# The expert gate is spread over the ranks by DMAs on the GpSimd queue in place of a matmul

## The reference

```python
def cond(x, weight, adapter_ids):                 # x: 8 sequences of 256 tokens, 1024 wide
    w = weight[adapter_ids]
    return jnp.einsum('bsi,boi->bso', x, w)

def ffn(x, W_base, b_base, W_router, A_stack, B_stack):
    xf = x.reshape(-1, 1024)
    probs = jax.nn.softmax(xf @ W_router.T, axis=-1)              # 8 experts
    topk_p, topk_i = jax.lax.top_k(probs, 2)
    topk_p = topk_p / jnp.sum(topk_p, axis=-1, keepdims=True)
    combine = jnp.sum(jax.nn.one_hot(topk_i, 8) * topk_p[..., None], axis=1)
    h = jnp.einsum('nd,erd->ner', xf, A_stack)                    # rank 16
    h = h * combine[..., None]
    lora_out = jnp.einsum('ner,eor->no', h, B_stack) * 2.0
    return xf @ W_base.T + b_base + lora_out

out = x + ffn(cond(x, cond_weight, ids), W_base, b_base, W_router, A_stack, B_stack)
```

## Time and profile before

| | us |
|---|---|
| median of 3 runs | 396.14 |
| lowest to highest | 395.95 to 396.31 |
| the profiled execution | 396.64 |
| its span, first to last instruction | 394.9 |
| PE busy | 389.8 (99%) |
| DVE busy | 306.1 (78%) |
| ACT busy | 183.9 (47%) |

### The profile page before, as it was taken

One profiled execution on the slowest core, in us unless ns is written; L12 is line 12 of the kernel. 1 busy time (PEld: TensorE's weight loads), 2 busy tenths in 40 slices (PEclk: granted clock), 3 DMA queues, 4 the chain that ended last, 5 costly groups with the idle time before them and its releaser, 6 DMA issues.

```text
span 394.9 us, 5710 instructions
## 1 busy us (share of the span) xinstructions
PE 389.8 (99%) x2189; PEld 332.8 (84%) x2189; DVE 306.1 (78%) x443; ACT 183.9 (47%) x282; POOL 40.1 (10%) x68
## 2 busy tenths in 40 slices
PE   7999999999999999999999999999999999999997
PEld 6888888888888888888888888888888888888886
DVE  4897967789699999984547786878867999999322
ACT  5877734749542334332146676357656223441000
POOL 0101100101000130021162000000000001301110
DMA  7998782768430136486669967347173102461222
GB/s 249 405 358 287 261 309 86 265 230 289 166 106 0 53 110 196 165 288 229 198 228 365 349 236 251 108 164 217 46 258 112 58 0 81 151 197 75 87 80 80
DMA packets 21227, 72.96 MB, mean 185 GB/s; under 512 B 2832, under 2 KB 3104, under 8 KB 21200
## 3 DMA queue, kind: packets, MB, share of 16 engines
q1 hardware_dynamic: 15984, 55.58, 40.8%
q0 software_dynamic: 4928, 15.97, 11.3%
q10 hardware_dynamic: 288, 1.05, 0.7%
HBM read 64.20 MB, written 8.39 MB: 184 GB/s over the span
## 4 chain that ended last, share of the span: by engine, by line
PE 97%; DMA 1%; SPq 1%; ACT 0%; issue 0%; DVE 0%
PE bank_x L829 30%; PE bank_x L833 15%; PE bank_y L814 9%; PE bank_y L815 8%; PE bank_y L816 8%; PE bank_x L816 8%; PE bank_x L814 8%; PE bank_x L815 8%; PE bank_y L873 2%; DMA raw<-w_cond 1%; SPq L368 1%; PE bank_y L893 0%; ACT wc_hl L501 0%; SPq L352 0%; DVE out_sb L606 0%
## 5 line engine op out<-in xcount | busy, mean ns | idle before, releaser
L829 PE MATMUL bank_x<-x_hl,wc_hl 128*128 128x512 f32 x512 | 128.7, 393 | 1.2 <-ACT wc_hl L501 1.2
L547 DVE TENSOR_TENSOR wc_hl<-raw,wc_hl 128x1024 fp32r<-128x1024 f32 x90 | 108.4, 1220 | 18.9 <-ACT wc_hl L483 18.8
L483 ACT CAST wc_hl<-raw 128x1024 fp32r<-128x1024 f32 x90 | 93.4, 1051 | 55.7 <-DVE raw L551 23.1
L829 PEld LDWEIGHTS bank_x<-x_hl,wc_hl 128*128 128x128 f32 x512 | 92.3, 189 | 18.3 <-ACT wc_hl L501 1.8
L833 PEld LDWEIGHTS bank_x<-x_hl,wc_hl 128*128 128x128 f32 x512 | 70.0, 190 | 5.1
L833 PE MATMUL bank_x<-x_hl,wc_hl 128*128 128x256 f32 x512 | 71.5, 282 | 0.0
L435 POOL DMA_DIRECT2D out<-out_sb x28 | 15.3, 545 | 249.8 <-DVE out_sb L598 228.5
L515 ACT COPY xc_low<-bank_x 128x256 f32<-128x256 f32 x64 | 23.6, 369 | 32.4 <-PE bank_x L833 32.3
L814 PE MATMUL bank_x<-x_hl,wc_hl 128*128 128x512 f32 x96 | 37.4, 389 | 0.0
L815 PE MATMUL bank_x<-x_hl,wc_hl 128*128 128x512 f32 x96 | 37.4, 389 | 0.0
L816 PE MATMUL bank_x<-x_hl,wc_hl 128*128 128x512 f32 x96 | 37.4, 389 | 0.0
(11 more groups left out here) (93 smaller groups left out, 492.8 us busy)
## 6 DMA issues: line engine op xcount, KB each, us to landing
raw<-w_cond SPq DMA_DIRECT2D x62, 512.0 KB, 4.9
raw<-w_base SPq DMA_DIRECT2D x24, 512.0 KB, 5.3
out_sb<-x POOLq DMA_DIRECT2D x32, 256.0 KB, 5.3
raw<-x SPq DMA_DIRECT2D x14, 512.0 KB, 4.6
out<-out_sb POOLq DMA_DIRECT2D x28, 256.0 KB, 2.3
raw<-x ACTq DMA_DIRECT2D x2, 512.0 KB, 3.6
raw<-w_cond SPq DMA_DIRECT2D x4, 256.0 KB, 3.8
out<-out_sb SPq DMA_DIRECT2D x3, 256.0 KB, 2.0
```

The source lines that it names most:

```text
L483: nc.scalar.copy(split_dst(key, HI), split_src(key)).then_inc(hi_done, 1)
L547: nc.vector.tensor_tensor(split_dst(key, LO), split_src(key), split_dst(key, HI).bitcast(F32), ALU.subtract).then_inc(lo_done, 1)
L829: nc.tensor.matmul(ps[:], wc_hl[:, slot_of(s, t), HI, k], x_hl[:, s % 2, k].rearrange("p h n -> p (h n)"), start=(k == 0), stop=False)
```

## The change

The gate is kept in one piece. DVE writes the scaled gate into gate_pad and transposes it into gate_cols; the split, the product with the mask, the matmul with `expand`, `expand` itself and its copy on ACT, and the wait of P2's last tile for h_gated are gone. In their place four DMAs for each pair, issued by POOL, copy 8 rows of gate_cols (128 tokens, 512 bytes a row) to 128 partitions of gate_rows, reading each row 16 times. POOL waits for the gate and, after the first pair, until the last pair's gate_rows have been used. gate_h waits for all four and reads gate_rows from SBUF. The warm-up matmuls at the start read h_hl, cleared to zero, in place of gate_rows.

```diff
-C_EXP, C_TRI, C_QUARTER = 0, P, P + EXPERTS * EXPERTS
-C_ALL = C_QUARTER + CG
+C_ALL = EXPERTS * EXPERTS
...
-        gate_rows = sb("gate_rows", [P, PTOK], F32R)
+        gate_rows = sb("gate_rows", [P, PTOK])
...
-        expand = sb("expand", [P, P], F32R)
-        gate_hl = sb("gate_hl", [P, NQ, NR], F32R)
+        gate_pad = sb("gate_pad", [P, NQ, NR])
...
+            def gate_to_rows(p):
+
+                pool.wait_ge(gate_ready, p + 1)
+                if p:
+                    pool.wait_ge(h_gated, p)
+                for j in range(CG):
+                    src = gate_cols[j * NR:j * NR + EXPERTS]
+                    nc.gpsimd.dma_start(gate_rows[:, j * P:(j + 1) * P],
+                                        src[:, None, :].broadcast_to([EXPERTS, RANK, P])).then_inc(gate_in, 16)
+
             for g in range(GROUPS):
                 for c in ("t1", "t2", "t3"):
+                    if c == "t3":
+                        gate_to_rows(2 * g)
                     for m in range(HT):
...
+                gate_to_rows(2 * g + 1)
                 for m in range(HT):
                     store(g, "C11", m)
...
-                        if (s, t) == (0, 6):
-                            act.wait_ge(consts_in, 16)
-                            nc.scalar.copy(expand[:], const_sb[:, C_EXP:C_EXP + P]).then_inc(expand_in, 1)
...
             def gate_h(p):
-                dve.wait_ge(gate_t_done, p + 1)
+                dve.wait_ge(gate_in, 16 * CG * (p + 1))
                 dve.wait_ge(h_copied, p + 1)
-                nc.vector.tensor_tensor(h_sb[:], h_sb[:], ps_tok[:], ALU.mult).then_inc(h_gated, 1)
+                nc.vector.tensor_tensor(h_sb[:], h_sb[:], gate_rows[:], ALU.mult).then_inc(h_gated, 1)
...
-                chain(nc.vector.scalar_tensor_tensor(gate[:], gate[:], SCALING, per_token(inv2), ALU.mult, ALU.mult))
-                ready()
                 if p == 0:
                     dve.wait_ge(gate_clear, 1)
-                chain(nc.vector.tensor_copy(gate_hl[:, :, 0:EXPERTS], gate[:]))
-                ready()
-                chain(nc.vector.tensor_tensor(gate_hl[:, :, EXPERTS:2 * EXPERTS], gate[:],
-                                              gate_hl[:, :, 0:EXPERTS].bitcast(F32), ALU.subtract))
-                ready()
-                chain(nc.vector.transpose(gate_cols, gate_hl[:].bitcast(F32).rearrange("p q n -> p (q n)")))
-                ready()
-                nc.vector.tensor_tensor(gate_rows[:].rearrange("p (j n) -> p j n", j=CG),
-                                        gate_cols[:, None].broadcast_to([P, CG, P]),
-                                        quarter[:, :, None].broadcast_to([P, CG, P]), ALU.mult).then_inc(gate_ready, 1)
+                chain(nc.vector.scalar_tensor_tensor(gate_pad[:, :, 0:EXPERTS], gate[:], SCALING, per_token(inv2),
+                                                     ALU.mult, ALU.mult))
+                ready()
+                nc.vector.transpose(gate_cols, gate_pad[:].rearrange("p q n -> p (q n)")).then_inc(gate_ready, 1)
...
-            def gate_to_rows(p):
-
-                if p == 0:
-                    pe.wait_ge(expand_in, 1)
-                pe.wait_ge(gate_ready, p + 1)
-                nc.tensor.matmul(ps_tok[:], expand[:], gate_rows[:], start=True, stop=True).then_inc(gate_t_done, 1)
-
...
-                elif j == P2 and m == 3:
-                    pe.wait_ge(h_gated, 2 * g + 2)
...
-                        if s % GSEQS == 2 and t == 1:
-                            gate_to_rows(2 * g)
                     if s % 2:
                         router(s // 2)
                         lora_down(s // 2)
-                second(g, P1)
-                gate_to_rows(2 * g + 1)
-                for j in (P2, P5, P6, P7, P4, P3):
+                for j in (P1, P2, P5, P6, P7, P4, P3):
                     second(g, j)
```

More of the change, by code:

```diff
@@ L249, in build @@
         stat = sb("stat", [P, 5, NQ])
-        quarter = const_sb[:, C_QUARTER:C_QUARTER + CG]
-        before = const_sb[:, C_TRI:C_TRI + EXPERTS * EXPERTS].rearrange("p (e j) -> p e j", e=EXPERTS)
+        before = const_sb[:].rearrange("p (e j) -> p e j", e=EXPERTS)
         bank_x = [psum(f"bank_x{m}") for m in range(HT)]
         bank_y = [psum(f"bank_y{m}") for m in range(HT)]
-        ps_logit, ps_h, ps_tok = bank_y[0], bank_y[1], bank_y[3]
+        ps_logit, ps_h, ps_warm = bank_y[0], bank_y[1], bank_y[3]
         consts_in = sem("consts_in")
         gate_clear = sem("gate_clear")
-        expand_in = sem("expand_in")
         bias_in = sem("bias_in")
@@ L279, in build @@
         gate_ready = sem("gate_ready")
-        gate_t_done = sem("gate_t_done")
+        gate_in = sem("gate_in")
         h_done = sem("h_done")
@@ L295, in build @@
         block = ctx.enter_context(nc.Block())
-        GATE_STEPS = 17
+        GATE_STEPS = 14
         def t_buffer(j):
@@ L417, in _ @@
         def _(pool):
-            nc.gpsimd.memset(gate_hl[:].bitcast(F32), 0.0).then_inc(gate_clear, 1)
+            nc.gpsimd.memset(gate_pad[:], 0.0).then_inc(gate_clear, 1)
             pool.wait_ge(cond_done, 3)
@@ L542, in _ @@
         def _(dve):
-            nc.vector.memset(gate_rows[:, 0:WARM_N].bitcast(F32), 0.0).then_inc(warm_clear, 1)
+            nc.vector.memset(h_hl[:, HI, 0, 0:WARM_N].bitcast(F32), 0.0).then_inc(warm_clear, 1)
             def lo(key):
@@ L957, in _ @@
             for _ in range(WARM):
-                nc.tensor.matmul(ps_tok[:, 0:WARM_N], gate_rows[:, 0:P], gate_rows[:, 0:WARM_N], start=True, stop=True)
+                nc.tensor.matmul(ps_warm[:, 0:WARM_N], h_hl[:, HI, 0, 0:P], h_hl[:, HI, 0, 0:WARM_N], start=True, stop=True)
             for g in range(GROUPS):
@@ L991 @@
     consts = np.zeros((P, C_ALL), np.float32)
-    row = np.arange(P) % NR
-    consts[:, C_EXP:C_EXP + P] = (row[:, None] < 2 * EXPERTS) & (row[:, None] % EXPERTS == np.arange(P)[None] // RANK)
-    consts[:, C_QUARTER:C_QUARTER + CG] = np.arange(P)[:, None] // NR == np.arange(CG)
-    consts[:, C_TRI:C_TRI + EXPERTS * EXPERTS] = (e[None, :] < e[:, None]).reshape(1, -1)
+    consts[:] = (e[None, :] < e[:, None]).reshape(1, -1)
     x_t = np.asarray(x).reshape(SEQS, TOK, 2, KT // 2, P).transpose(0, 2, 4, 3, 1)
```

## The result

The changed kernel takes 406.38 us (median of 5 runs, 405.98 to 406.53) against 396.14 before (median of 5 runs, 395.95 to 398.45). The ratio is 1.0251, with a 95% interval of 1.0239 to 1.0263: slower by 2.5%. The profiled executions, 406.38 and 396.64 us, differ by 9.7, as do their spans, 404.6 and 394.9; the profiled execution of before was 0.5 above its median.

What follows compares the result with a forecast made beforehand. PE bounds the kernel, busy 389.8 of 394.9 us. The first gate's wait costs +9.4, three other removed matmuls give -0.69: +8.7, so 404.9 us against the median 396.14; range 401.0 to 408.4.

Steps and rivals of the forecast that it cites:

- The queue: POOL, first gate of group 0: gate DMAs stand behind the eighth residual load, so the first starts at 77.95 us.
- The landing: First pair's gate DMAs: the fourth, started at 79.57, lands 3.5 us later, at 83.07; bounds 2.3 and 7.0.
- The trace is above that rule: DMA landings: the skill's rule would give 2.6 us for 256 KB, where load rows have 3.1 to 7.0.
- The chain behind the multiply: DVE and ACT from 73.5 to 90.2 us: one chain behind gate_h, which moves as a whole, 10.28 us late.
- The rival that DVE makes up ground: Between 83 and 100 us DVE and ACT catch up, PE loses only at (2,7): +5.1, 401.3 us; chance 10%.
- The smallest lead: PE at stage (3,3): lead only 0.88 us, because of lora_b's split and difference; PE starts it 9.4 us late.
- The other gates: Other three gates: DMA time hidden, 5.1 us against 9.5 at group 0's second and 10.1 available at group 1's first.
- The removed matmuls: PE: four gate matmuls of 0.23 us each go, 0.92 us; one counted within the +9.4, three as -0.69.
- The clock: PE's clock falls after a gap; two slow stages would end at 102.4, +2.0, 406.9 us; chance 8%.
- one slow stage is swallowed: PE at (2,7): a slow stage, 85.62 to 91.2, then three more until 99.6, still before (3,3) at 100.37.
- The gap of 0.9 that I expected before (3,0): PE reaches (3,0) at 88.41 but waits until 89.29 for the low half of x(3,1): another 0.9 us.
- The rival on the other side: First gate_h: DVE never waits, -0.9, 395.2 us; PE loses nothing if the gate lands before 73.67; chance 4%.

Runs made afterwards that it cites:

- behind seven loads: Changed kernel with the first pair's gate DMAs placed after seven of POOL's residual loads in place of eight; 402.13 us, ratio 1.0146.
- behind five: Changed kernel with the first pair's gate DMAs placed after five of POOL's residual loads in place of eight; 395.42 us, ratio 0.9980.
- with the matmul: Kernel before, without gate DMAs, its first gate_h also waiting for POOL's eighth residual load to land; 403.44 us, ratio 1.0184.
- the move: Changed kernel with lora_b's load, split and difference moved eight steps ahead, to (1,5) and (1,6); 404.38 us, ratio 1.0212.
- behind six: Changed kernel with the first pair's gate DMAs placed after six of POOL's residual loads in place of eight; 396.92 us, ratio 1.0020.
- the kernel with the late multiply: Changed kernel, queue unchanged, with group 0's first gate multiply and what follows it five steps later; 395.49 us, ratio 0.9976.
- the filled kernels: Changed kernel with idle matmuls in PE's gaps: 28 before (2,7), median 407.47 us; also 8 before (3,3), 406.41 to 408.28 us.

## Why the prediction was right

It said 404.9 us, with a range from 401.0 to 408.4, slower with 95%. Step by step, on the profiled execution:

- *The queue.* Right. The eighth residual went out at 77.06 (I had 77.23), the first gate DMA at 77.75 (77.95). An issue took 0.61 us and not 0.54; the fourth began near 79.57, where I had it.
- *The landing.* This is the term that was too small: up to 4.3 us, where I took 3.5 between the rows of 3.1 and 3.9. The multiply started at 83.94, not 83.07. It is the whole miss of the mechanism, 0.9 us. The Trainium skill's "DMA: Bandwidth & Descriptors", section "Anatomy of one DMA — SWDGE (gpsimd) path", puts a transfer at about 2.0 us plus its bytes at 436 GB/s, an estimate of 2.15 us for such a copy. The trace disagrees: no landing of a gate DMA in it, at any of the four gates, was under 3.5, so the rows of loads were the better guide. "The trace is above that rule" was too wide, though: the stores, 2.3 us for 256 KB, lie under the estimate of 2.6 that it gives for them. My reason for a short landing, that DVE stands, holds only in part. With the DMA engines 0.54 busy the landings took up to 4.3, and up to 7.8 with DVE running on and the engines 0.99 busy. But DVE stood behind seven loads too, and they took up to 6.0; it ran on behind five, and they took up to 4.3. So the landings go with how busy the DMA engines are. That a standing DVE lowers this only once the loads on their way have ended is how I read it; no run tests it.
- *The chain behind the multiply.* Right: two operations 5 and 17 us behind it are late by 11.15 and 11.16. The rival that DVE makes up ground is out.
- *The smallest lead.* Right. Predicted 0.88 at (3,3); measured 11.15 - 10.33 = 0.82 here, 0.80 with the matmul and 0.81 behind seven loads. Its cause, lora_b, is shown by the move: the gap goes with it.
- *The other gates.* Hidden, as said. The removed matmuls: 10.33 - 0.69 = 9.64 against 9.7 between the spans; behind five loads, where they are all that is left, 0.8.
- *The clock.* A rival at 8%, of which the part "one slow stage is swallowed" came true: clock 0.50, stage (2,7) 2.1 us longer, nothing lost. I should have expected it rather than allowed for it: "TensorE: Matmul & The Clock Gate" of the Trainium skill says in its section "Part 1: The HAM clock gate" that an idle TensorE goes to the lower clock, and the trace agrees. The gap of 0.9 that I expected before (3,0) isn't there, since the slow stage filled it.
- *The rival on the other side.* Its bound, a multiply that starts by 73.67, fits: behind five loads it starts at 71.92 and PE has no gap, behind six at 74.16 and PE has one. No run has it closer to the bound.

The median is 1.5 us above the forecast. The landing is 0.9 of it, and some 0.5 is that the profiled execution of before, from whose rows I worked, lay above its median.

## What to carry to other kernels

A DMA that is added to a queue inherits every wait ahead of it: before putting one there, set the time at which the queue reaches it against the time at which its consumer needs it, and move one or the other (both gave 0.2% gain in place of 2.5% loss). Where a helper engine has no slack to make up ground, as here, its stall costs the main engine the stall less the smallest lead found anywhere behind it, and not less the lead at the next wait. In the traces here a slow clock after a gap cost time only where no later wait of PE was standing anyway.

## What the hardware showed that I had not expected

- The landing of four 64 KB copies within SBUF on POOL's queue went with the other traffic: 3.6 to 4.3 us with the DMA engines 0.54 busy (from 77.5 to 84) in the changed kernel and 0.58 behind five loads (61.9 to 68), 4.3 to 5.8 at 0.86 behind six (66.5 to 72.5), 5.4 to 6.0 at 0.82 behind seven (72 to 80), 6.0 to 7.8 at 0.99 in the kernel with the late multiply (77.5 to 84). No run changes the traffic alone.
- PE's clock went down to 0.50 in a gap of 7.2 us, and (2,7) was as slow (3.78 us for its wide matmuls) after the gap of the kernel with the late matmul, listed as 3.20. Behind seven loads, in the profiled execution, (2,7) was slow (4.17 us, to 86.41) after a gap listed as 2.55 and (3,3) after one listed as 1.77, and the clock fell only when PE was running again: 1.00 up to 83.5 and 0.59 in the half microsecond behind it, 1.00 up to 97.0 and 0.75 behind it. The other three runs, with mean clocks of 0.995 to 0.996 against 0.991, had about half of that.
- The same kernel can have such a fall in one execution and none in the next: one run in ten behind six loads, two in four and one in four in the filled kernels, each about 2 us longer than the others.
